# Slots without an edge get an index past the table, and the gathers get a bounds check that skips them

## What is computed

```python
h = jnp.maximum(_layernorm(x), 0.0)
# layer 0
anchor_adj = jnp.einsum('md,de,ne->mn', h, weight, input)
atten = softmax(where(adj > 0, anchor_adj, NEG_PAD) / 0.07, axis=1)
x = x + atten @ input
h = jnp.maximum(_layernorm(x), 0.0)
# layer 1 (N = 6144)
hw = h @ W
e = leaky_relu((hw @ a_src)[:, None] + (hw @ a_dst)[None, :], 0.2)
valid = (adj > 0) & (hw.sum(axis=1) != 0)[None, :]
att = where(valid, softmax(where(valid, e, -1e9), axis=1), 0.0)
attention = where(att >= 1e-4, att, 0.0) * L[:, None]      # L = valid entries of the row
x = x + elu(hw + attention @ hw)
```

## Time and profile before

| | us |
|---|---|
| median of three runs | 753.84 |
| lowest and highest | 750.98, 756.42 |
| profiled execution, its own time | 758.33 |
| its span, first to last instruction | 756.7 |

### The profile page before, as it was taken

One profiled execution on the slowest core, in us unless ns is written; L12 is line 12 of the kernel. 1 busy time (PEld: TensorE's weight loads), 2 busy tenths in 40 slices (PEclk: granted clock), 3 DMA queues, 4 the chain that ended last, 5 costly groups with the idle time before them and its releaser, 6 DMA issues.

```text
span 756.7 us, 9557 instructions
## 1 busy us (share of the span) xinstructions
PE 413.3 (55%) x2947; PEld 276.4 (37%) x2947; DVE 521.8 (69%) x1921; ACT 410.8 (54%) x424; POOL 366.3 (48%) x424
## 2 busy tenths in 40 slices
PE   3433646566667676767675846647360520416654
PEld 1010213244444343435352524426260520415654
DVE  0019596889898988979893958949822532639994
ACT  4458677777878788888856758662300110012122
POOL 5000140607070606151573765748887887878700
PEclk9577787788988899879795879976565555566786
DMA  8999799999999999999999999932121232223422
GB/s 326 430 412 419 262 305 352 341 352 319 351 353 334 363 336 348 357 349 332 371 321 290 319 306 321 336 110 57 38 59 46 57 76 52 44 58 88 124 83 74
DMA packets 37478, 186.78 MB, mean 247 GB/s; under 512 B 7856, under 2 KB 8112, under 8 KB 18864
## 3 DMA queue, kind: packets, MB, share of 16 engines
q1 hardware_dynamic: 28208, 167.02, 58.8%
q0 software_dynamic: 9216, 19.11, 12.0%
HBM read 179.73 MB, written 6.37 MB: 246 GB/s over the span
## 4 chain that ended last, share of the span: by engine, by line
DVE 30%; POOL 21%; DMA 18%; issue 12%; ACT 9%; PE 8%; SPq 0%; POOLq 0%; DVEq 0%; ACTq 0%
DMA arena<-in_adj 18%; POOL arena L819 12%; ACT arena L873 7%; PE K L1424 4%; POOL mean_w L814 3%; DVE keys L1029 2%; POOL E L819 2%; POOL X L790 2%; DVE s_e L1136 1%; POOL arena L790 1%; DVE mi_w L1175 1%; DVE RTp L1194 1%; PE G L1635 1%; ACT R_all L902 1%; DVE G L1135 1%
## 5 line engine op out<-in xcount | busy, mean ns | idle before, releaser
L873 ACT ACTIVATE arena<-arena,half_c 128x2048 bf16<-128x2048 int32 x144 | 284.5, 1999 | 88.0 <-DMA arena<-in_adj 77.2
L790 POOL DMA_INDIRECT X<-in_L_gnn_input,idx_all x132 | 131.8, 998 | 299.7 <-DVE idx_near L1108 233.9
L1424 PE MATMUL K<-arena,bits 128*128 128x512 bf16 x576 | 174.0, 443 | 22.6 <-ACT arena L873 22.4
L819 POOL DMA_INDIRECT arena<-table,idx_near x96 | 99.5, 1036 | 28.5 <-issue 22.2
L1424 PEld LDWEIGHTS K<-arena,bits 128*128 128x128 bf16 x576 | 60.2, 110 | 97.3 <-ACT arena L873 31.0
L1029 DVE MAX8 keys<-K 128x8 int32<-128x128 f32 x192 | 42.4, 281 | 56.7 <-PE K L1424 56.7
L1422 PE MATMUL K<-key_add,key_one 128*128 128x512 bf16 x48 | 22.4, 466 | 57.8 <-DVE keys L1029 32.1
L819 POOL DMA_INDIRECT E<-table,idx_near x48 | 47.0, 979 | 14.4 <-issue 12.2
L1436 PE MATMUL G<-g,R_all 128*128 128x128 bf16 x324 | 25.3, 228 | 39.3 <-DVE s_e L1136 26.0
L1099 DVE COPY led<-SA 128x396 f32<-128x396 f32 x12 | 6.8, 570 | 56.0 <-PE SA L1482 56.0
L814 POOL MEMSET mean_w<- 128x512 f32 x72 | 38.5, 535 | 2.1
(11 more groups left out here) (245 smaller groups left out, 1031.6 us busy)
## 6 DMA issues: line engine op xcount, KB each, us to landing
arena<-in_adj SPq DMA_DIRECT2D x144, 1024.0 KB, 9.3
table<-hs SPq DMA_DIRECT2D x12, 262.0 KB, 9.1
hs<-table SPq DMA_DIRECT2D x12, 262.0 KB, 2.8
E<-in_L_gnn_input SPq DMA_DIRECT2D x1, 3072.0 KB, 23.9
out_x<-x_all SPq DMA_DIRECT2D x12, 256.0 KB, 2.1
x_all<-in_x SPq DMA_DIRECT2D x1, 2560.0 KB, 17.4
X<-in_L_gnn_input,idx_all POOLq DMA_INDIRECT x132, 6.0
arena<-table,idx_near POOLq DMA_INDIRECT x96, 2.7
```

Source lines behind the costliest of these rows:

```text
L790: pool.indirect_dma_start(out=x_of(b)[:, e, :], out_offset=None, in_=inp, in_offset=bass.IndirectOffsetOnAxis(ap=idx_all[:, at:at + 1], ax ...
L819: pool.indirect_dma_start(out=E[g][:, t, :], out_offset=None, in_=tables[g], in_offset=bass.IndirectOffsetOnAxis(ap=idx_near[:, t, g:g + 1 ...
L873: nc.scalar.activation(sign[:, load % RING, :], ring[:, load % RING, :], ACT.Sign, bias=half_c[:], scale=1.0).then_inc(signed, 1)
L1424: last = mm(bank_[:], bits[:, third * TB + j, :], sign[:, load % RING, j * FOLD:(j + 1) * FOLD], start=False, stop=(third == G - 1 and j = ...
```

## The change

Empty slots get an index past the end of the table, and every gather gets a bounds check (`bounds_check=N - 1` or `THIRD - 1`, `oob_is_err=False`) that passes over such slots. `columns_of_edges` adds 2N to `idx_f` where it is 0, with two more linked DVE instructions on 128 x 12 elements. A slot that is passed over keeps what was in its place, so the places are cleared once: `X` and the ends of `E0` and `arena` at the start, and the last three words of each record (`no_record(g)`) before the first gather of each third.

```diff
+        no_edge = sb("no_edge", [P, BG])
@@ POOL, start, after memset(cum) and before memset(hs)
+                pool.memset(X[:], 0.0)
+                pool.memset(E0[:].rearrange("p t c -> p (t c)")[:, T * D:T * REC], 0.0)
+                pool.memset(arena[:, RING * THIRD * 3 // 2:2 * T * REC], 0.0)
@@ neighbours(b, first, last)
-                            in_offset=bass.IndirectOffsetOnAxis(ap=idx_all[:, at:at + 1], axis=0)
+                            in_offset=bass.IndirectOffsetOnAxis(ap=idx_all[:, at:at + 1], axis=0),
+                            bounds_check=N - 1, oob_is_err=False
@@ records(g, first, last)
-                            in_offset=bass.IndirectOffsetOnAxis(ap=idx_near[:, t, g:g + 1], axis=0)
+                            in_offset=bass.IndirectOffsetOnAxis(ap=idx_near[:, t, g:g + 1], axis=0),
+                            bounds_check=THIRD - 1, oob_is_err=False
+                def no_record(g):
+                    link(pool.memset(E[g][:, :, D:REC], 0.0))
@@ POOL's order: after third_stored(0), third_stored(1), third_stored(2)
+                no_record(0)        # in turn n == EARLY
+                no_record(1)
+                no_record(2)
@@ columns_of_edges(b), DVE
-                    ts(idx_all[:, edges(b)], idx_f[:, 0:n_e], 1.0, -1.0, ALU.max, ALU.add)
+                    link(ts(no_edge[:, 0:n_e], idx_f[:, 0:n_e], 0.0, 2.0 * N, ALU.is_equal, ALU.mult))
+                    link(tt(idx_f[:, 0:n_e], idx_f[:, 0:n_e], no_edge[:, 0:n_e], ALU.add))
+                    ts(idx_all[:, edges(b)], idx_f[:, 0:n_e], -1.0, None, ALU.add)
```

## The result

The changed kernel takes 757.32 us in the median of 20 runs (754.75 to 760.23), the kernel before 752.74 in 20 runs of the same kind (746.09 to 757.11). The ratio is 1.0081, with a 95% interval of 1.006 to 1.0101: slower by 0.8%, within the 1% that was called no change, and 0.7 us from the forecast of 758. The time came out as forecast, but not by the sum that led to it: POOL's row of gathers cost some 17 us more than it has for it, the loading half gained some 19 us more, and the two errors cancel. That they are of one size is luck.

What follows compares the result with a forecast made beforehand. It took DMA to bound bands 8 to 11 and POOL's issuing of gathers the stretch from 505 us. Terms 2.8 + 0 + 0.6 - 2 + 2.6 = +4.0 us took the median 753.84 to 758 us, range 742 to 785.

Steps and rivals of the forecast that it cites:

- the likeliest case: The forecast's own sum holding, within 1% of before: 758 us, own range 751 to 763, chance 0.40.
- Two DVE instructions: Index tables ready 0.40 us later each band; counted in six DVE-bound bands and after the last load: +2.8 us.
- The side effect: DVE's L1175 slowed beside POOL's L801 in the loading bands; both move together, so 0, at most 9 us in six.
- Memsets at the start: Clearing `X` (2.8 us) and the two ends (some 0.4 us) is hidden by 38 us of streaming: 0.
- `no_record`: Clearing record ends on POOL, 0.3 us each; one falls in idle time, two in POOL's row of gathers: +0.6 us.
- Fewer rows moved: Bands 9 to 11, bound by DMA: a third of slots unfetched; bounds nothing to 14.8 us, taken as -2 us.
- The price of a gather on POOL: The check lengthens each of 132 gathers on the path by 0.02 us: +2.6 us, bounds -41 to +125 us.
- rival 1: The check makes every POOL gather longer: 775 us at +0.15 us each, 796 at +0.31; chance 0.35.
- rival 3: DMA is relieved evenly in the loading bands: 7.6 to 14.8 us gained in place of 2, 745 to 752 us; chance 0.10.
- Rival 2: Skipped rows shorten the gather on POOL: 735 us at -0.15 us each, 714 at the whole bound; chance 0.12.
- Rival 4: Nothing is skipped in effect, rows are fetched as dummies: the sum without -2, 760 us; chance 0.03.

## Why the prediction was right, and where it was not

The time, the range and the likeliest case (within 1% of before) were right. The sum of +4.0 us met the measured +4.6 by luck, since two errors cancel: -18.6 us in the loading half, for which the sum has +0.8, and +20.0 in POOL's row, for which it has +3.2. Against the second profile of the kernel before the two are -19.7 and +23.6. (A small misreading, without effect: the band from 295.09 to 334.31 us takes 39.2 us; 39.0 is the mean of five.)

*Two DVE instructions, +2.8 us.* They are there, and cost 0.4 us a band, but the five bands from 177.51 to 371.48 didn't get longer: 38.8 us each in place of 39.0. The side effect that was counted at 0 offsets them. In the kernel before L1175 and L1177 lost 2.5 us a band beside POOL's tensor operations. Six checked gathers are 0.3 us longer, so L806 comes later against DVE and meets other instructions. The changed kernel, DVE by line from 177.51 to 371.48 us:

```profile
L1054 DVE TENSOR_SCALAR col_i<-keys 128x128 int32<-128x128 int32 x5 | 6.5, 1305 | 0.0
L1201 DVE TENSOR_TENSOR d_e<-s_e,mie 128x12 f32<-128x12 f32 x5 | 4.3, 861 | 0.2
...
L1192 DVE TENSOR_TENSOR mi<-mi_w,mi 128x8 bf16<-128x8 f32 x5 | 0.8, 168 | 0.2
L1190 DVE TENSOR_TENSOR mi_w<-mi 128x8 f32<-128x8 f32 x5 | 0.8, 167 | 0.2
```

and the kernel before, from 177.99 to 372.99 us:

```profile
L1175 DVE TENSOR_TENSOR mi_w<-mi 128x8 f32<-128x8 f32 x6 | 10.4, 1730 | 0.2
...
L1177 DVE TENSOR_TENSOR mi<-mi_w,mi 128x8 bf16<-128x8 f32 x5 | 5.6, 1111 | 0.2
...
L1041 DVE TENSOR_SCALAR col_i<-keys 128x128 int32<-128x128 int32 x5 | 1.1, 220 | 0.0
...
L1186 DVE TENSOR_TENSOR d_e<-s_e,mie 128x12 f32<-128x12 f32 x5 | 0.9, 171 | 0.2
```

The stall left the two small instructions (L1190 and L1192 take 0.17 us now) and came back at L1054 and L1201: 1.1 and 0.7 us a band. In all 0.7 us a band less, against 0.4 more: that fits the bands' 0.2 us. It is an account of DVE's time and not of what bounds a band in every run: with the check alone DVE is busy 162.7 us in these five bands in place of 170.8, and they take 202.8 us in place of 195.0.

*Memsets at the start, 0.* Right: that of `X` took 2.65 us, forecast 2.8, and nothing waited for it; the first L806 came at 136.85 us, before it was 137.51. *`no_record`, +0.6.* Each is 0.24 us, with a gap of 0.77 behind it where before there was one of 0.27 after the pause; about right.

*Fewer rows moved, -2 us.* The term that failed by most in this half. Bands 9 to 11 alone got 17.1 us shorter (13.9 against the second profile of before). What the skipped rows have of it is shown by two pairs that differ in them (and in DVE's two instructions): 130.5 to 122.1 us with the moves, 130.8 to 122.6 with registers, from one profile a version and on different chips. That is 8.2 to 8.4 us, at the lower end of the 7.6 to 14.8 that were worked out for an even relief, and some four times the -2 that was taken. The step that failed is the choice near the lower bound. It rested on rows of low partitions remaining with their engines and setting the end of each load; the two versions that skip by partition give 123.6 and 122.1 us, so that relief of the high partitions alone is worth as much as one spread over all. The Trainium skill's rule on the descriptor swizzle ("DMA: Bandwidth & Descriptors"), by which engines 8 to 15 write partitions 64 to 127, so that only they would be relieved, isn't refuted as to who writes what, which no row shows; but the gain near 0 that was derived from it is.

In the bands ahead of these, which have no record gathers, the rows aren't shown to do anything. Skipping makes them 242.1 to 234.6 us long with the moves and 230.1 to 228.9 with registers, 7.5 and 1.2 us less, where the two profiles of the kernel before have 235.5 and 240.3. By the ratios skipping is 2.7% (21 us) of the whole kernel with the moves and 1.2% (9 us) with registers. And the 8 us hold with the pauses as they are: without them the version that skips takes 137.4 us in bands 9 to 11, the kernel before 135.2.

*The rest of it stays open.* Checked gathers without skipping shorten bands 9 to 11 by 5.5 to 9 us, with moves and with registers alike. With registers the bands ahead are 5 to 10 us shorter too, with moves they are 2 to 7 us longer. Two things change with the check: gathers come 4% further apart, and POOL's tensor operations fall on other DVE instructions. The second fits the bands ahead in the version with registers: from 181.06 to 372.27 us DVE is busy 166.4 us, 4.4 less than before, and the five bands take 191.2 us, 3.8 less. It doesn't fit the check with moves, as said above. For the first speak bands 9 to 11 of the versions that skip and have fewer pauses, against it the same bands of the kernel before without pauses; no run changes the distance of two gathers alone.

*The price of a gather on POOL, +2.6 us.* Here the working was furthest off: +20 us. Two steps of it. First, +0.02 us for the check was taken from a comparing fill; it is 1.00 - 0.945 = 0.055 us, on the 126 gathers in POOL's row 6.9 us. Second, and worth twice that, the sum had no term for an instruction that the check brings along outside the gather. That is 0.5 us of gap behind each pause, `add_mean` or `no_record` in POOL's row, 28 of them: 14 us. The text gave the point from which rival 1 would decide as 0.05 us a gather; the price was 0.16 us a gather, so rival 1 came true in size (20.0 us, almost the 21 that it said for 0.15), though two thirds of the price stand in gaps and not in the gather, and rival 3 together with it. The text weighed them as alternatives, and they act in different halves of the kernel. Rival 2 is refuted, since a gather that skips 43 rows takes as long as one that skips none. Rival 4 is refuted by 12.82 MB.

## What to carry to other kernels

Cost an added argument of an instruction also by what it adds to the queue ahead of it: a bound given as a number became a register move per gather, and cost 2.5% of the kernel by standing between a wait and the gather; from a register set once it leaves no gap. Skipping rows saves transfer time and no issue time, so it paid where the DMA engines are full, and its check cost where the issuing engine is; where a kernel has both kinds of stretch the two halves have to be priced as terms of one sum, not as rivals. Such a gain also hangs on how closely the transfers are issued: with the same rows skipped the same bands took 122.6, 131.3 and 137.4 us as the pauses got fewer. A sum that meets the time is not yet right: only the stretches show whether its terms are.

## What the runs showed of the hardware

- A gather of 128 rows with a bounds check occupies POOL for 1.00 us, without one for 0.945, whether rows are skipped or not.
- A gather behind a register move that carries a wait starts 0.77 us after what it waits for, without the move 0.27 us.
- Empty slots all reading one row made the gathers' packets longer (12.0% of the engines' time against 9.9% when spread) but did not lengthen the bands.
- DVE instructions of 0.17 us took 1.7 and 1.1 us beside tensor operations on POOL, and the loss moves from one to another when POOL's order shifts by 0.3 us.
- Gathers issued without a break for tens of microseconds leave PE, DVE and ACT nearly idle (7.6 us of DVE work in 80 us); two memsets behind every fourth, 1.13 us, keep them running (54.7 us of DVE work in 86). The cause is open.
